# A kernel of linear attention and a mixture of experts: group 1's totals elsewhere, unread products in the head, and a last group in another order

## The reference, cut to what matters

```python
q, k, v = heads(x @ Wq.T + bq), heads(x @ Wk.T + bk), heads(x @ Wv.T + bv)   # 16 heads of 8
q, k = exp(q), exp(k)
num = einsum('zsD,zsDd->zsd', q, cumsum(k[..., None] * v[..., None, :], axis=1))
den = sum(q * cumsum(k, axis=1), axis=-1)
x = layernorm(x + (num / den) @ Wo.T + bo)
# experts: 32 of 64 hidden units each, sigmoid scores, the best 2 of 4 expert groups, of them the best 8 experts,
# weights normalised and times 2.5; out = sum_e w_e * down_e(silu(gate_e x) * up_e x)  +  shared(x), 128 hidden units
x = layernorm(x + experts(x) + shared(x))
```

## Time and profile before

| | us |
|---|---|
| median of three executions | 462.77 |
| the profiled execution | 463.29 |
| its span in the profile | 461.5 |
| PE busy | 424.0 (92%) |
| DVE busy | 347.4 (75%) |
| POOL busy | 282.4 (61%) |
| ACT busy | 273.3 (59%) |

### The profile page before, as it was taken

How to read it: one execution, slowest core, us unless ns; L and a number is a source line. 1 busy time by engine, 2 the same in 40 slices (tenths; PEclk the granted TensorE clock), 3 DMA queues, 4 the chain that set the end, 5 groups by cost and what they waited for, 6 DMA issues and landing times.

```text
span 461.5 us, 10791 instructions
## 1 busy us (share of the span) xinstructions
PE 424.0 (92%) x3954; PEld 324.8 (70%) x3954; DVE 347.4 (75%) x909; ACT 273.3 (59%) x530; POOL 282.4 (61%) x208
## 2 busy tenths in 40 slices
PE   5855799999999999999999999999999999899982
PEld 3733587778867787778877787778877787578761
DVE  2678548797878968797878968796878968777652
ACT  3835334963587546963587546963587546555642
POOL 2565236864676557864677557764677557757781
PEclk9989589999999999999999999999999999999996
DMA  7400544346440823446340923446440913466500
GB/s 233 187 1 1 147 92 90 92 97 141 93 113 7 197 69 82 91 103 135 91 116 12 202 68 74 90 104 134 91 116 9 200 41 81 91 134 129 121 11 23
DMA packets 28660, 45.08 MB, mean 98 GB/s; under 512 B 1984, under 2 KB 10304, under 8 KB 28224
## 3 DMA queue, kind: packets, MB, share of 16 engines
q1 hardware_dynamic: 28608, 44.40, 41.2%
HBM read 41.77 MB, written 2.62 MB: 96 GB/s over the span
## 4 chain that ended last, share of the span: by engine, by line
PE 40%; DVE 32%; issue 12%; POOL 8%; ACT 2%; DVEq 1%; ACTq 0%; POOLq 0%
PE bank L326 39%; DVE units L866 7%; POOL units L958 5%; DVE stats L741 2%; DVE hidden_lo L721 2%; POOL rstd L977 2%; DVE top_of_group L782 2%; DVE x L753 2%; DVE bank L775 1%; ACT hidden_hi L584 1%; DVE replaced L814 1%; DVE out_sb L878 1%; DVE k_sum L847 1%; DVE probs L731 1%; DVE kv_blocks L836 1%
## 5 line engine op out<-in xcount | busy, mean ns | idle before, releaser
L958 POOL TENSOR_TENSOR units<-units,weight_wide 128x512 f32<-128x512 f32 x128 | 174.3, 1367 | 130.5 <-DVE units L866 115.9
L602 ACT ACTIVATE units<-bank 128x512 f32<-128x512 f32 x136 | 80.7, 594 | 79.2 <-PE bank L326 78.9
L866 DVE TENSOR_TENSOR units<-bank,units 128x512 f32<-128x512 f32 x136 | 92.9, 683 | 35.1 <-PE bank L326 28.0
L584 ACT ACTIVATE hidden_hi<-units 128x512 fp32r<-128x512 f32 x136 | 86.1, 634 | 53.7 <-POOL units L958 47.7
L721 DVE TENSOR_TENSOR hidden_lo<-units,hidden_hi 128x512 fp32r<-128x512 f32 x112 | 97.7, 873 | 19.6 <-ACT hidden_hi L584 18.8
L326 PE MATMUL bank<-x_hi,gate_hi 128*128 128x512 f32 x136 | 62.1, 457 | 2.0 <-DVE units L866 1.6
L326 PE MATMUL bank<-hidden_hi,down_hi 128*128 128x512 f32 x136 | 55.0, 404 | 1.7 <-DVE hidden_lo L721 1.7
L326 PE MATMUL bank<-x_hi,up_hi 128*128 128x512 f32 x136 | 54.7, 403 | 1.8 <-ACT units L602 1.8
L326 PE MATMUL bank<-x_lo,gate_hi 128*128 128x512 f32 x136 | 54.6, 401 | 0.0
L326 PE MATMUL bank<-x_hi,gate_lo 128*128 128x512 f32 x136 | 54.4, 400 | 0.0
L326 PE MATMUL bank<-x_hi,up_lo 128*128 128x512 f32 x136 | 54.1, 398 | 0.0
(11 more groups left out here) (107 smaller groups left out, 670.8 us busy)
## 6 DMA issues: line engine op xcount, KB each, us to landing
weight_wide<-weight_d SPq DMA_DIRECT2D x62, 512.0 KB, 6.7
xT<-xT_in SPq DMA_DIRECT2D x8, 256.0 KB, 6.8
x_tok<-x_in SPq DMA_DIRECT2D x8, 256.0 KB, 6.9
out_dram<-out_sb SPq DMA_DIRECT2D x8, 256.0 KB, 2.3
weight_wide<-up_in SPq DMA_DIRECT2D x1, 1088.0 KB, 9.0
up_raw<-up_in SPq DMA_DIRECT2D x1, 1088.0 KB, 11.0
down_raw<-down_in SPq DMA_DIRECT2D x1, 1088.0 KB, 13.2
weight_d<-weightT SPq DMA_DIRECT2D x8, 64.0 KB, 1.6
```

What stands on the lines that cost most here:

```text
L584: nc.scalar.activation(hidden_hi[place(n, g)][:, :], units[place(n, g)][:, :], ACT.Copy).then_inc(hidden_hi_done, 1)
L602: nc.scalar.activation(units[place(n, g)][:, :], up_banks[2 * n % 3][:, :], ACT.Silu).then_inc(silu_done, 1)
L866: V.tensor_tensor(units[place(n, g)][:, :], up_banks[(2 * n + 1) % 3][:, :], units[place(n, g)][:, :], ALU.mult).then_inc(gated_done, 1)
L958: G.tensor_tensor(units[place(n, g)][:, :], units[place(n, g)][:, :], weight_wide[:, (n - 1) % (2 * PIECE), :], ALU.mult).then_inc(hidden_ ...
```

## The change

- **Second totals.** `k_totals(1)` moves from slot 8 of the head's mid steps to slot 14 of them, behind routing and the first two gated products; `q_times_totals(1)` on GpSimd from slot 10 to 13. For f > 1 `masked_states(f)` moves from slot 15 to 14, ahead of `k_totals(f)`.
- **Unread products.** `keep_warm(count)` issues products of 256 columns of `attn_w` into `y_bank`, which nobody reads: 6, 2, 4, 3, 2 and twice 1, at places of the head (`WARM`).
- **Splits.** gate_lo and up_lo are made in an early part (9 blocks) and a late one; the early part of both comes first. `ready_blocks` gives high and low part of group 0's block 0 to slot 2 instead of 1.
- **Order in a slot.** The gate products of the router stand behind `down(n - LAG)` in slot 10; in the last group with mid steps but no front (g = 6), `turn_exponentials` goes to slot 11.
- **POOL_LOWS** gets block 12.
- **Last group.** Its blocks are taken in the order 1 to 16, 0 (`block_at`), with the loads of the last two pieces in slots 4 and 7 instead of 5 and 9. Its tail goes by halves: two copies yT, transposes into two banks, `last_rows` on VectorE, tiles 2 and 3 scaled on VectorE, two stores.

```diff
@@ -25,9 +25,13 @@
...
 RING = 4
+EARLY_BLOCKS = 9
+EARLY_COLS, LATE_COLS = slice(0, 128 * EARLY_BLOCKS), slice(128 * EARLY_BLOCKS, 128 * BLOCKS)
+WARM = {"x1": 6, "x1T": 2, "up": 1, "weight": 4, "den": 3, "between": 2}
+HALVES = (slice(0, GROUP // 2), slice(GROUP // 2, GROUP))
...
 FIRST_BLOCKS = (slice(0, 1), slice(1, 2), slice(2, 4))
-POOL_LOWS = (9, 10, 11)
+POOL_LOWS = (9, 10, 11, 12)
@@ -199,9 +203,13 @@
...
-            if g == 0 and n in (2, 3):
-                return (1, 2) if n == 3 else ()
+            if g == 0 and n in (1, 2, 3):
+                return ((), (0,), (1, 2))[n - 1]
...
+
+        def block_at(n, g):
...
+            return n if g < GROUPS - 1 else (n + 1) % BLOCKS
@@ -255,7 +263,14 @@
...
                     sp.dma_start(down_raw, down_d).then_inc(down_loaded, 16)
-                if tail and n == 8:
+                if g == GROUPS and n == 8:
+                    for h, (done, count) in enumerate(((last_done, 1), (out_done, 2 * GROUPS - 1))):
+                        tiles, at = slice(2 - 2 * h, 4 - 2 * h), (GROUPS - 1) * GROUP + 256 * (1 - h)
+                        sp.wait_ge(done, count)
+                        sp.sem_inc(apart, 1)
+                        sp.dma_start(out_d[at:at + 256, :].rearrange("(a p) c -> p a c", p=128),
+                                     out_sb[:, tiles, :]).then_inc(out_stored, 16)
+                if tail and n == 8 and g < GROUPS:
@@ -263,8 +278,9 @@
...
                                  out_sb[:, :, :]).then_inc(out_stored, 16)
-                if ffn and n in (5, 9):
-                    load_wide(2 + (n - 5) // 4, g, u)
+                late = (5, 9) if g < GROUPS - 1 else (4, 7)
+                if ffn and n in late:
+                    load_wide(2 + late.index(n), g, u)
@@ -334,10 +350,10 @@
...
                     pe.wait_ge(x1_lo_done, reached(g + 1))
-                if g == 0 and n == 0:
-                    pe.wait_ge(gate_split, 2)
-                    pe.wait_ge(up_split, 2)
-                cols = slice(128 * n, 128 * n + 128)
+                if g == 0 and n in (0, EARLY_BLOCKS):
+                    pe.wait_ge(gate_split, 2 if n == 0 else 3)
+                    pe.wait_ge(up_split, 2 if n == 0 else 3)
+                cols = slice(128 * block_at(n, g), 128 * block_at(n, g) + 128)
@@ -365,11 +381,16 @@
...
                     pe.wait_ge(y_copied, reached(g))
-                cols, h = slice(128 * n, 128 * n + 128), place(n, g)
+                cols, h = slice(128 * block_at(n, g), 128 * block_at(n, g) + 128), place(n, g)
...
+
+            def keep_warm(count):
...
+                for _ in range(count):
+                    mm(y_bank[:, 0:256], wqT, attn_w[:, 0:256])
@@ -420,20 +441,24 @@
...
                     down(BLOCKS - LAG, g - 1)
+                if ffn and g == 0 and n in (1, 2):
+                    keep_warm(WARM["up"])
...
                     down(BLOCKS - LAG + n, g - 1)
+                if ffn and n >= LAG:
+                    down(n - LAG, g)
...
+                    if m == 0:
+                        keep_warm(WARM["x1T"])
...
                     last.then_inc(gate_ready, 1)
-                if ffn and n >= LAG:
-                    down(n - LAG, g)
-                if mid and not front and n == 10:
+                if mid and not front and n == (10 if m == 0 else 11):
@@ -443,11 +468,17 @@
...
                     for i in range(TILES):
-                        last = nc.tensor.transpose(work_bank[:, 128 * i:128 * i + 128],
+                        if t == GROUPS - 1 and i == TILES // 2:
+                            pe.wait_ge(y_copied, GROUPS + 1)
+                        bank = o_bank if t == GROUPS - 1 and i >= TILES // 2 else work_bank
+                        last = nc.tensor.transpose(bank[:, 128 * i:128 * i + 128],
...
-                    last.then_inc(y_turned, 1)
+                        if i == TILES - 1 or t == GROUPS - 1 and i == TILES // 2 - 1:
+                            last.then_inc(y_turned, 1)
...
                     pe.wait_ge(qk_sum_done, reached(m + 1))
+                    if m == 1:
+                        keep_warm(WARM["den"])
@@ -465,6 +496,8 @@
...
                 if mid and n == 2:
+                    if m == 1:
+                        keep_warm(WARM["between"])
@@ -487,6 +520,8 @@
...
                 if mid and n == 9:
+                    if m == 0:
+                        keep_warm(WARM["x1"])
@@ -535,6 +570,8 @@
...
                 if mid and n == 14:
+                    if m == 0:
+                        keep_warm(WARM["weight"])
@@ -575,10 +612,10 @@
...
-                if n == 0:
-                    act.wait_ge(gated_done, reached(BLOCKS * g + 1))
+                if block_at(n, g) == 0:
+                    act.wait_ge(gated_done, reached(BLOCKS * g + n + 1))
...
-                    act.wait_ge(hidden_done, reached(ROUTED * g + n))
+                    act.wait_ge(hidden_done, reached(ROUTED * g + block_at(n, g)))
@@ -590,7 +627,8 @@
...
                     act.wait_ge(y_turned, reached(t))
-                    nc.scalar.activation(yT[:, :], y_bank[:, :], ACT.Copy).then_inc(y_copied, 1)
+                    for c in (HALVES if t == GROUPS - 1 else (slice(0, GROUP),)):
+                        nc.scalar.activation(yT[:, c], y_bank[:, c], ACT.Copy).then_inc(y_copied, 1)
@@ -681,7 +719,7 @@
...
-                if tail and n in OUT_SLOTS:
+                if tail and n in OUT_SLOTS and (g < GROUPS or n == OUT_SLOTS[0]):
@@ -856,6 +894,35 @@
...
+            def last_rows(t, u):
...
+                dve.wait_ge(out_stored, reached(16 * t))
+                dve.wait_ge(rstd2_done, t)
+                dve.wait_ge(shift2_done, t)
+                for h, c in enumerate(HALVES):
+                    tiles = slice(2 * h, 2 * h + 2)
+                    dve.wait_ge(y_turned, t + 1 + h)
+                    V.tensor_tensor(out_sb[:, tiles, :].rearrange("p a c -> p (a c)"), (work_bank, o_bank)[h][:, c],
+                                    x1[u][:, tiles, :].rearrange("p a c -> p (a c)"), ALU.add
+                                    ).then_inc(resid2_done, 1)
+                    dve.wait_ge(resid2_done, t + 2 + h)
+                    for i in (2 * h, 2 * h + 1):
+                        last = V.bn_stats(stats2[:, i, :], out_sb[:, i, :])
+                    last.then_inc(ln2_chain, 1)
+                dve.wait_ge(ln2_chain, NORM_LINKS * t + 2)
+                dve.sem_inc(apart, 1)
+                for i in range(TILES):
+                    last = V.bn_aggr(mean_var2[:, i, :], stats2[:, i, :])
+                last.then_inc(ln2_chain, 1)
+                dve.wait_ge(ln2_chain, NORM_LINKS * t + 3)
+                V.tensor_scalar(var2[:, :], mean_var2[:, :, 1], LN_EPS, None, ALU.add).then_inc(var2_done, 1)
+                V.tensor_scalar(neg_mean2[:, :], mean_var2[:, :, 0], -1.0, None, ALU.mult).then_inc(neg_mean2_done, 1)
+                dve.wait_ge(rstd2_done, t + 1)
+                for i in (2, 3):
+                    last = V.tensor_scalar(out_sb[:, i, :], out_sb[:, i, :], mean_var2[:, i, 0:1], rstd2[:, i:i + 1],
+                                           ALU.subtract, ALU.mult)
+                last.then_inc(last_done, 1)
@@ -883,6 +950,8 @@
...
                     V.tensor_scalar(neg_mean2[:, :], mean_var2[:, :, 0], -1.0, None, ALU.mult).then_inc(neg_mean2_done, 1)
+                if g == GROUPS and n == 4:
+                    last_rows(g - 1, 1 - u)
@@ -901,6 +970,8 @@
...
                     normalise(x1[1 - u], resid, mean_var, rstd1, x1_done)
+                if front and f > 1 and n == 14:
+                    masked_states(f)
@@ -908,9 +979,9 @@
...
                     last.then_inc(first_masked, 1)
-                if m == 0 and mid and n == 8:
+                if m == 0 and mid and n == 14:
...
-                if front and f != 1 and n == 15:
+                if front and f == 0 and n == 15:
@@ -940,6 +1011,12 @@
...
+            def weight_lows(low, raw, high, split, cols):
...
+                pool.wait_ge(split, 1)
+                G.tensor_tensor(low[:, cols], raw[:, cols], high[:, cols].bitcast(F32), ALU.subtract
+                                ).then_inc(split, 1)
@@ -948,15 +1025,15 @@
...
                 m, f = g + 1, g + 2
-                if ffn and n >= 1:
...
-                    if g == 0 and n - 1 in (0, 1, 2):
-                        pool.wait_ge(first_loaded[n - 1], 32)
-                    elif (n - 1) % PIECE == 0:
-                        pool.wait_ge(wide_loaded[(n - 1) // PIECE], loads_of((n - 1) // PIECE, g + 1))
+                if ffn and block_at(n, g) > 0:
+                    w = block_at(n, g) - 1
+                    if g == 0 and w in (0, 1, 2):
+                        pool.wait_ge(first_loaded[w], 32)
+                    elif w % PIECE == 0:
+                        pool.wait_ge(wide_loaded[w // PIECE], loads_of(w // PIECE, g + 1))
...
```

(16 more changed lines are left out.)

10 lines of the change are left out of this document (5 added, 5 removed).

## The result

The kernel after takes **469.1 us** (median of 4 executions, 468.55 to 469.63), the kernel before beside it on the same chip 462.95: ratio 1.0124, 95% interval 1.0098 to 1.015. The change made the kernel slower, where 451.8 us were forecast. The profiled execution took 469.44 us, its span is 467.7 us (before 461.5).

The account below looks back on a forecast made before the run. It took TensorE, busy 92%, to bound the kernel's middle, with gains where it idles or runs slowly. Terms -8.2 - 2.1 - 0.2 - 0.45 = -10.95 us gave 451.8 us; range 449.3 to 457.0.

Parts of the forecast that it names:

- six products "cover 2.6 of the 3.29 us idle, at no cost": Head, first TensorE gap: six unread 256-column products at x1, 0.43 us each, fill idle time at no cost.
- SP's queue has nothing new in between: Head: the weights' write to memory goes 3.8 us earlier, all loads behind it, with nothing new in SP's queue.
- Head, -8.2: Head to second state product: scans leave routing's path and TensorE keeps full clock, 8.2 us less.
- Rivals 1 and 3: Head: clock falls anyway, 457.7 us, chance 0.11; scans collide with down_lo in their new place, 456.1 us, chance 0.03.
- All groups, -2.1 and -0.2: All groups: earlier masked states remove waits at next scores, 2.1 us less; gate products behind down product, 0.2 us less.
- rival 2: All groups: the 0.5 us gaps only change owner, gated product and maskings as late; 453.9 us, chance 0.10.
- Block 12, 0: Behind multiply 13: block 12's low part moves from VectorE to GpSimd, 1.29 us each, counted as nothing.
- Rival 4: Slot 13, all groups: GpSimd's added low part delays multiply 14 onward, TensorE loses 1.65 us in 8 groups; 467.1, chance 0.04.
- the exponentials' slot +0.4: Group 6: the transpose of exponentials one slot later comes behind nine more products, 0.4 us more.
- +1.35 and -1.15 for the turned order: Group 7: first block waits for routed weights, delaying the yT copy, 1.35 us more; last down product ends 1.15 us earlier.
- Tail, -1.05: Kernel's end: halves overlap copy, transposes and statistics, and ScalarE and VectorE share the scaled tiles, 1.05 us less.

## Why the prediction was wrong

**The step that failed** is in the part on the head: six products "cover 2.6 of the 3.29 us idle, at no cost", and likewise for the others. I costed them by the columns that they compute. Their 76 entries in TensorE's instruction stream were never counted, and neither was the queue that brings them. That term was 0 in the sum and measured +12.8 us (469.1 against 456.26 with the same products and the burst split). None of the four rivals has this mechanism. What I wrote of SyncE, "SP's queue has nothing new in between", was true of what it issues; the loads moved nowhere harmful for the data, but they are what a fetch waited behind in these traces. The rest of the miss, 3.75 us of span (-7.2 with the burst in two parts, -10.95 forecast), is in the steps below.

The Trainium skill (Runtime: NRT & Kernel Launch, section "Instruction fetch mechanics") says that the sequencer drives its own DMA queue to fetch the next 256 instructions while it runs the current ones, and that the fetch is hidden by the rate at which instructions are issued. The trace agrees with the blocks: 3992 matmuls and 3992 weight loads are 31.2 times 256, and q8 has 32 packets (before 30.9 and 31). It doesn't agree with "hidden", and the measurement decides: the stops of 1.61, 3.21 and 1.87 us.

By the other steps, with the burst in two parts, where the change shows itself without stops (span 454.3, 7.2 under before, where I had forecast 10.95):

- **Head, -8.2**: measured -8.03 at the second state product, and all of it stands at the weights of group 1; 0.58 of it is the start, where nothing was changed (the very first scores at 13.16 for 13.74). Right in mechanism and nearly in size, the routing's start too (32.02 for some 32.1; in after, which started later, 32.81). Rivals 1 and 3 did not come: PEclk stayed at 1.00 through the head, and the scans took 1.26 us (VectorE's timeline in after):

```profile
32.81 0.30 DVE L812 TENSOR_SCALAR bank<-bank 128x128 f32<-128x128 f32 x1 [2.70 <-PE bank L437]
43.71 1.26 DVE L885 TENSOR_TENSOR_SCAN k_sum<-kT 128x256 f32<-128x256 f32 x2
```

  How the 8 us divide is known only roughly: in the six profiled kernels without products the second state product comes between 56.18 and 58.75, as the clock happened to fall, so the reordering alone gives 3.3 to 5.8 and the clock that the products hold 2.2 to 4.8.
- **All groups, -2.1 and -0.2**: nothing came (5 periods, 258.47 before, 258.42 now). This is rival 2, which I gave 0.10: the gated product was as late. TensorE stood still only 0.52 us in a period, and I took 0.35 of it although I had listed what was late next.
- **Block 12, 0**: right in groups 1 to 5, where it costs nothing (in after's order it saves 0.16 us of the period), and wrong in the last two. Rival 4 had the mechanism (multiply 14, high part, gated product 16) and nearly the size, 1.65 for 1.72 us, but put it in all eight groups; it came in the last two, which have no masked states to make.
- **Last groups**: the exponentials' slot +0.4, measured +0.3. The period up to the weights of group 7 is +0.57 in all. From there to the last yT I had +1.35 and -1.15 for the turned order and nothing for block 12, +0.2; measured +1.47.
- **Tail, -1.05**: measured -1.15 (from the turn of yT to the end of the span 8.87, now 7.72). VectorE and ScalarE share the tiles as forecast (timelines of the end of after, four engines):

```profile
463.10 1.01 POOL L1044 TENSOR_TENSOR rstd<-var,neg_half 128x4 f32<-128x4 f32 x1 [7.26 <-DVE var L918]
464.14 0.60 DVE L922 TENSOR_SCALAR out_sb<-out_sb,mean_var,rstd 128x128 f32<-128x128 f32 x2 [1.05 <-POOL rstd L1044]
464.42 0.88 ACT L727 ACTIVATE out_sb<-out_sb,shift,rstd 128x128 f32<-128x128 f32 x2 [4.34 <-POOL shift L1049]
464.84 0.92 SPq L271 DMA_DIRECT2D out_dram<-out_sb  x2
```

Sum: -8.0 - 0.05 + 0.57 + 1.47 - 1.15 = -7.2, as the spans say.

## What to carry to other kernels

Instructions are not free because their engine is idle: in this long unrolled program each one moved every later fetch against the work around it, and a fetch that came only behind a burst of loads on all 16 DMA engines stopped TensorE, and in two of three places its clock fell behind. So look at the instruction queue and at the "issue" waits in the profile of a program with thousands of matmuls, count how many instructions are left when a late fetch lands, and leave gaps between long loads; here splitting one burst in two turned 1.2% slower into 1.5% faster. Work that is moved to another engine for the steady state should be judged anew in the last groups, where that state has ended.

## What was not expected of the hardware

- A fetch of 16 KB for TensorE takes about 1 us once it runs (210.90 to 211.98), but in after it came 3.2 to 5.0 us later against the scores than with small or split loads, behind loads at some 210 GB/s. Where TensorE had run dry it resumed 1.3 to 1.6 us behind the landing.
- The sensitivity: 20 more instructions were enough for a stop of 1.24 us, 36 for 3.68, 76 for 3.21, while 140 and 204 gave none in the full groups. The trace of before shows how near it was. Two of its fetches begin as a burst ends, at 111.00 and at 214.21 us:

```profile
0.00:111.00 111.00, 90.83 (x1079) 68.10 (x1080) 76.97 (x195) 59.80 (x114) 57.36 (x38) 0.91 0.42 112
0.00:214.21 214.21, 193.00 (x2068) 147.37 (x2069) 161.68 (x421) 126.12 (x246) 124.03 (x88) 0.95 0.43 106
```

  TensorE had made 2159 and 4137 matmuls and weight loads by then, 31 and 61 short of the 2190 and 4198 at which the changed kernels ran dry; some 10 more pass while a fetch runs. So 20 and 36 added instructions use up the first margin and not the second (stops up to 107.8 and 107.0, none at 210), and 76 use up the second (the stop at 210). In after no stop stands at 2190, because with 76 added the same fetch ran at 99.94, 1933 matmuls and loads into the stream and ahead of the burst. A shift can thus be judged in good part from the profile of before; that this would have named the stops in advance is not shown by a run made for it.
- 64 semaphore instructions at the start of TensorE's program cost 4.5 us, 128 cost 14.7. Why they are so dear there was not tried.
- Of the stop near 60 us, in group 0, its place in the stream and its cure are shown (the runs with the burst in two parts have none, small loads from group 1 on leave it); why it is 4.10 us long with 64 empty instructions was not taken apart further.
